# Eight of the 32 stencil groups summed by TensorE in a PSUM bank, the other 24 by VectorE

## What is computed

```
x = x + deformable_conv(group_norm(x))     # 8 groups of 16 channels, 9 sampling points per group
t = t + attention(layer_norm(t))           # 4 sequences of 1024 tokens
t = t + mixture_of_experts(layer_norm(t))  # top 2 of 8 experts, gelu
```

```
samples = _bilinear_sample(img, sg)        # at 9 offset points
out = (samples * m).sum(-1)                # m: softmax over the 9 points
return out @ out_w + out_b
```

## Time and profile before

| | |
|---|---|
| median of 3 runs | 685.37 us (684.22 to 685.88) |
| profiled execution, own time | 684.17 us |
| its span (first to last instruction) | 682.3 us |
| mean granted TensorE clock | 0.937 |
| busy: TensorE / VectorE / ScalarE / GpSimd | 86% / 83% / 34% / 50% |

### The profile page before, as it was taken

How to read it: one execution, slowest core, us unless ns; L and a number is a source line. 1 busy time by engine, 2 the same in 40 slices (tenths; PEclk the granted TensorE clock), 3 DMA queues, 4 the chain that set the end, 5 groups by cost and what they waited for, 6 DMA issues and landing times.

```text
span 682.3 us, 11125 instructions
## 1 busy us (share of the span) xinstructions
PE 587.8 (86%) x3518; PEld 435.4 (64%) x3518; DVE 565.8 (83%) x1028; ACT 234.0 (34%) x343; POOL 338.8 (50%) x407
## 2 busy tenths in 40 slices
PE   5989969888879588689786779999999999989995
PEld 4567556565556465466564667767777778775774
DVE  4679999999999699789999999956777667654877
ACT  6064405307116107006207000144454444414431
POOL 7505794888578658748667960201222121114222
PEclk9889959999899789969979889999999999999998
DMA  7096403003003006000000000000000000004111
GB/s 190 34 344 216 130 0 108 4 3 110 0 2 111 0 1 251 22 1 3 0 1 4 1 1 1 0 1 1 1 1 1 1 0 1 1 1 125 40 39 47
DMA packets 26238, 30.71 MB, mean 45 GB/s; under 512 B 5572, under 2 KB 18324, under 8 KB 26196
## 3 DMA queue, kind: packets, MB, share of 16 engines
q1 hardware_dynamic: 24094, 29.77, 13.3%
q0 software_dynamic: 1408, 0.36, 0.6%
q10 hardware_dynamic: 694, 0.01, 0.1%
HBM read 25.07 MB, written 5.05 MB: 44 GB/s over the span
## 4 chain that ended last, share of the span: by engine, by line
PE 38%; POOL 15%; DVE 15%; DMA 14%; issue 12%; POOLq 3%; ACT 1%; DVEq 1%; SPq 0%; ACTq 0%
DMA got<-padded,cell_now 11%; PE banks L1013 9%; PE pair L993 8%; DVE prod L1605 7%; POOL got L1258 6%; PE pair L1081 4%; PE banks L1003 4%; PE banks L1119 4%; PE banks L894 4%; DVE stencil L1546 2%; POOL cell_now L1254 2%; PE pair L838 2%; DMA padded<-stage 1%; POOL place L1337 1%; POOLq L1314 1%
## 5 line engine op out<-in xcount | busy, mean ns | idle before, releaser
L894 PE MATMUL banks<-ident,prod 128*128 128x128 f32 x1440 | 219.7, 295 | 63.5 <-DVE prod L1605 61.8
L894 PEld LDWEIGHTS banks<-ident,prod 128*128 128x128 f32 x1440 | 174.1, 150 | 125.3 <-DVE prod L1605 101.1
L1605 DVE TENSOR_TENSOR prod<-shifted,stencil 128x1024 f32 (+3 forms) x208 | 216.0, 1079 | 0.1
L1363 POOL TENSOR_TENSOR rstd_now<-mv_now,neg_half 128x2 f32<-128x2 f32 x32 | 23.0, 718 | 119.0 <-DVE mv_now L1656 119.0
L838 PE MATMUL pair<-xg,dw_diag 128*128 128x512 f32 x144 | 73.9, 614 | 1.4 <-DVE xg L1417 1.4
L1258 POOL DMA_INDIRECT got<-padded,cell_now x44 | 63.6, 1446 | 19.0 <-issue 10.1
L1013 PEld LDWEIGHTS banks<-shifted 128*128 128x128 f32 x512 | 60.2, 192 | 8.1 <-issue 6.1
L1013 PE MATMUL banks<-shifted 128*128 128x128 f32 x512 | 63.3, 277 | 2.3 <-ACT shifted L714 1.4
L993 PE MATMUL pair<-shifted 128*128 128x512 f32 x128 | 60.6, 596 | 0.1
L1671 DVE TENSOR_REDUCE neg_max<-pair 128x1 f32<-128x1024 f32 x32 | 39.2, 1224 | 23.1 <-PE pair L993 22.0
L1538 DVE TENSOR_TENSOR outer<-hats 128x800 f32<-128x800 f32 x56 | 56.1, 1001 | 1.2
(11 more groups left out here) (250 smaller groups left out, 920.7 us busy)
## 6 DMA issues: line engine op xcount, KB each, us to landing
shifted<-padded SPq DMA_DIRECT2D x42, 256.0 KB, 4.0
shifted<-padded SPq DMA_DIRECT2D x14, 640.0 KB, 8.5
res<-in_x_dram SPq DMA_DIRECT2D x4, 512.0 KB, 6.2
padded<-stage SPq DMA_DIRECT2D x4, 512.0 KB, 11.2
stage<-in_L_ffn_W_dram SPq DMA_DIRECT2D x16, 128.0 KB, 2.2
out_dram<-res SPq DMA_DIRECT2D x16, 128.0 KB, 1.8
got<-padded,cell_now POOLq DMA_INDIRECT x44, 3.0
padded<-stencil SPq DMA_DIRECT2D x2, 228.0 KB, 2.6
```

Source lines behind the costliest of these rows:

```text
L894: mm = pe.matmul(acc_of(c, r), prod[:, slot, r * G:(r + 1) * G, :].rearrange("p g c -> p (g c)"), ident[:, :], is_transpose=True, start=(t ...
L1605: ins = ve.tensor_tensor(prod[:, dx:dx + n, :, :], shifted[:, dx:dx + n, bass.ds(((c % HALF) * ROWS + dy) * G, ROWS * G), :], stencil_of[: ...
```

## The change

The groups 24 to 31 of a chunk (`SUMMED` = 8) are no longer added by VectorE. VectorE still computes all outer products, for all 32 groups. After each it waits for the product and raises `outer_done`; TensorE then adds the product of the eight groups into PSUM bank 2 with an fp32 matmul against the identity, at the window of the point (`sum_point`). In front of point 0 a matmul with a zero vector opens the bank. Each sum raises `outer_read`, which VectorE waits for before it writes `outer` again. When nine are done, ScalarE copies the bank into the stencil (`copy_sums`) and raises `stencil_summed`, and VectorE waits for that before the first product of the chunk. VectorE's adds cover 24 groups (`DIRECT`). The units that stood between product and add now stand behind the add. ScalarE clears 24 groups only.

```diff
 
 
 POINT_FILL = (1, 2, 2, 2, 2, 2, 2, 2, 2)
-STENCIL_FILL = (0, 0, 0, 0, 0, 0, 0, 0, 2)
+FIRST_POINT = BEGIN + 5
+POINT_UNIT = [FIRST_POINT + sum(POINT_FILL[:q]) for q in range(PTS)]
+SUMMED = 8
 
 EXP_AT = 4
 
...
         y_new = over_prod[:, 2:4, :].rearrange("p s (t c) -> p s t c", c=C)
         b2_rows = over_prod[:, 0, :].rearrange("p (n c) -> p n c", n=B)
         dense_t = over_prod[0:E, 1, :].rearrange("e (n t) -> e n t", n=B)
+
+        DIRECT = ROWS * G - SUMMED
+        size = ROWS * G * TAPS * TAPS
+        spare = prod[:, :, :, :].rearrange("p s g c -> p (s g c)")
+        first_outer = [outer[:, :, :, :]] + [spare[:, i * size:(i + 1) * size].rearrange("p (g a b) -> p g a b", a=TAPS, b=TAPS)
+                                             for i in range(3)]
+        summed = bank[2][:, 0:SUMMED * STENCIL]
 
         def key_bank(j):
 
...
 
             silu(0)
 
-            def prepare(k, exp_at=EXP_AT):
+            def copy_sums(k):
+                sc.wait_ge(outer_read, (k + 1) * PTS)
+                sc.sem_inc(act_waited, 1)
+                sc.activation(stencil[:, bass.ds(k % 2, 1), DIRECT * STENCIL:].rearrange("p s g -> p (s g)"),
+                              summed, ACT.Copy).then_inc(stencil_summed, 1)
+
+            def prepare(k, exp_at=EXP_AT, sums_at=TAPS):
 
                 sc.wait_ge(off_mm, k + 2)
                 if not isinstance(k, int) or k > 0:
...
                 sc.wait_ge(off_done, k + 1)
                 sc.sem_inc(act_waited, 1)
                 for t in range(TAPS):
+                    if t == sums_at:
+                        copy_sums(k - 1)
                     if t == exp_at:
                         sc.wait_ge(logits_done, k + 1)
                         sc.sem_inc(act_waited, 1)
...
 
                 sc.wait_ge(prod_done, (k + 1) * NEAR)
                 sc.sem_inc(act_waited, 1)
-                sc.activation(stencil[:, bass.ds(k % 2, 1), :].rearrange("p s g -> p (s g)"),
-                              zero_col[:, 0:1].to_broadcast([P, ROWS * G * STENCIL]), ACT.Copy
+                sc.activation(stencil[:, bass.ds(k % 2, 1), 0:DIRECT * STENCIL].rearrange("p s g -> p (s g)"),
+                              zero_col[:, 0:1].to_broadcast([P, DIRECT * STENCIL]), ACT.Copy
                               ).then_inc(stencil_clear, 1)
 
             def count_out(k):
...
             signs_of(0)
             silu(1)
             count_out(0)
+            copy_sums(0)
             prepare(1)
             signs_of(1)
             silu(2)
             count_out(1)
 
             def turn(j, conv_ahead):
-                prepare(j + 2)
+                prepare(j + 2, sums_at=3)
                 clear_stencil(j)
                 signs_of(j + 2)
                 if conv_ahead:
...
                               bank[at][:, n0 * P:n1 * P].rearrange("p (n c) -> p n c", c=C), ACT.Copy
                               ).then_inc(res1_first if n0 == 0 else res1_done, 1)
 
+            copy_sums(CHUNKS - 1)
             copy_out(CHUNKS - 2)
             copy_out(CHUNKS - 1)
             for i, k in enumerate((CHUNKS - 2, CHUNKS - 1)):
...
                                    start=False, stop=(i == 3))
                 mm.then_inc(far_mm, 1)
 
+            def sum_point(k, q):
+
+                kx, ky = q // 3, q % 3
+                if q == 0 and k > 0:
+                    pe.wait_ge(stencil_summed, k)
+                pe.wait_ge(outer_done, PTS * k + q + 1)
+                if q == 0:
+                    pe.matmul(summed, ones16[0:1, :], zero16[0:1, 0:1].to_broadcast([1, SUMMED * STENCIL]),
+                              start=True, stop=False)
+                    src = stencil_of[:, k % 2, DIRECT:, 0:TAPS, 0:TAPS]
+                else:
+                    src = (first_outer[q % 4] if k == 0 else outer)[:, DIRECT:, :, :]
+                pe.matmul(summed.rearrange("p (g a b) -> p g a b", a=WIN, b=WIN)[:, :, ky:ky + TAPS, kx:kx + TAPS],
+                          ident[:, :], src, start=False, stop=(q == PTS - 1)).then_inc(outer_read, 1)
+
             def acc_of(c, r):
                 return bank[1 + 2 * (c % 2)][:, r * P:(r + 1) * P]
 
...
             for t in range(9):
                 convolve(1, t)
             count_far(0)
-            keep_clock(20, bank[2])
+            for q in range(6):
+                sum_point(0, q)
+                keep_clock(4, bank[3])
             offsets(1, 0, ROWS)
-            keep_clock(14, bank[2])
+            for q in range(6, PTS):
+                sum_point(0, q)
+                keep_clock(3, bank[3])
             add_up(0, 0, first_of(BEGIN))
+
+            point_taps = [first_of(u) for u in POINT_UNIT]
 
             def turn(k, first, conv_ahead):
                 for i in range(first_of(BEGIN), NEAR):
...
                     r, between = divmod(i - AT_OFFSETS, 2)
                     if 0 <= r < ROWS and between == 0 and conv_ahead:
                         offsets(k + 2, r, r + 1)
+                    if i in point_taps:
+                        sum_point(k + 1, point_taps.index(i))
                     add_up(k, i, i + 1)
                 add_up(k, NEAR, NEAR + first_of(BEGIN))
 
...
                         list_far(k)
                     if q == AT_SILU and silu_next:
                         finish_silu(k + 1)
+                    if q > 0:
+                        ve.wait_ge(outer_read, PTS * k + (q if q > 1 else 0))
                     own(ve.tensor_tensor(to if q == 0 else outer[:, :, :, :],
                                          hy[:, :, q, :].unsqueeze(3).to_broadcast(full),
                                          hx[:, :, q, :].unsqueeze(2).to_broadcast(full), ALU.mult))
+                    own.wait()
+                    ve.sem_inc(outer_done, 1)
+                    if q == PTS - 1:
+                        ve.sem_inc(hats_used, 1)
+                    if q > 0:
+                        to = to[:, 0:DIRECT, :, :]
+                        own(ve.tensor_tensor(to, to, outer[:, 0:DIRECT, :, :], ALU.add))
                     fill(POINT_FILL[q])
-                    if q > 0:
-                        own.wait()
-                        if q == PTS - 1:
-                            ve.sem_inc(hats_used, 1)
-                        own(ve.tensor_tensor(to, to, outer[:, :, :, :], ALU.add))
-                        fill(STENCIL_FILL[q])
                 own.wait()
 
             def first_stencils():
...
                 point_product(1)
                 for q in range(1, PTS):
                     if q + 1 < PTS:
+                        if q >= 4:
+                            ve.wait_ge(outer_read, q - 2)
                         point_product(q + 1)
                         ve.wait_ge(dve, own.base + own.n - 1)
                     else:
                         own.wait()
                         ve.sem_inc(hats_used, 1)
+                    ve.sem_inc(outer_done, 2 if q == 1 else 1)
                     if q == AT_LIST:
                         list_far(0)
                     if q == AT_SILU:
                         finish_silu(1)
-                    own(ve.tensor_tensor(place_of_point(q), place_of_point(q), held[q % 4], ALU.add))
+                    to = place_of_point(q)[:, 0:DIRECT, :, :]
+                    own(ve.tensor_tensor(to, to, first_outer[q % 4][:, 0:DIRECT, :, :], ALU.add))
                 own.wait()
 
             def list_far(k):
...
                     full = [P, n, ROWS * G, CG]
                     if u == 0:
                         ve.wait_ge(rows_ready, c + 1)
+                        ve.wait_ge(stencil_summed, c + 1)
                     ve.wait_ge(prod_free, c * NEAR + max(freed_by(t), freed_by(t + n - 1)) + PROD)
                     ins = ve.tensor_tensor(
                         prod[:, dx:dx + n, :, :],
```

11 lines of the change are left out of this document (6 added, 5 removed).

## The result

| | before | after |
|---|---|---|
| median of 4 runs each | 684.92 us (684.22 to 685.88) | 694.06 us (692.58 to 695.48) |
| ratio, 95% interval | | 1.014, 1.0121 to 1.0159 |
| span of the profiled execution | 682.3 us | 690.7 us |
| VectorE's MAX8 for chunks 0 / 5 / 7 starts at | 54.61 / 292.11 / 387.81 | 52.84 / 295.98 / 396.39 |
| GpSimd takes the list of chunk 4 | 290.31 | 276.17 |

The forecast was 685.0 us (681.0 to 690.5). The change is slower, and by more than the range allowed.

What follows compares the result with a forecast made beforehand. GpSimd was taken to bound the stage before 292 us, VectorE alone from there to 435. VectorE's +1.4 us and GpSimd's -1.8 gave -0.4 us: from the median 685.4 to 685.0 us, range 681 to 690.5.

Steps and rivals of the forecast that it cites:

- What bounds before: Deformable convolution: GpSimd's far points are the clock before 292 us, VectorE alone from there to 435 us.
- The adds: VectorE's adds over 24 groups: 0.21 us less each, eight adds in each of eight chunks.
- The new order: VectorE, add directly behind its product: exposed gap 0.13 us instead of 0.03, so a point saves 0.11 us net.
- the row with one additional wait: Profile row of VectorE's gap before the gate, 0.13 us, taken as the gap between product and add.
- The wait at the chunk's end: VectorE's first product of a chunk waits for ScalarE's copy: about 1.8 us in turns 0 to 5, ends 1.0 and 3.
- waits for TensorE in the loop: VectorE waiting for TensorE before outer products in the loop: named as making the forecast wrong, given no size.
- The sum of a turn: A full VectorE turn: 0.9 us shorter from adds and order, 1.8 us longer from the wait for the copy.
- The start: Chunk 0: sums replace filler matmuls, VectorE's first product starts 4 us later, weighing of the hats +5.4 us.
- Where VectorE meets the lists: VectorE 1.9 us late at the first far-point list, 3.2 us of waiting left at the second; sum +1.4 us.
- GpSimd's own path: GpSimd's steps beside VectorE's new gaps and idle time: -1.8 us, at least 3 us uncertain either side.
- The rivals: Alternatives to the forecast of no change: slower, 688 to 691 us, chance 0.31; faster, 680 to 683 us, chance 0.29.
- The slower one: TensorE's sums become the bound, chunk-end wait 3 us instead of 1.8: 688 to 691 us, chance 0.31.

Runs made afterwards that it cites:

- tenth experiment: The kernel before with only VectorE's adds cut to 24 groups, old order, the other eight groups' sums left out: 679.0 us, ratio 0.9918.
- first experiment: The changed kernel, but ScalarE copies the summed groups before its copy of the offsets: 679.5 us, ratio 0.9927 to the kernel before.

## Why the prediction was wrong, step by step

**What bounds before: right.** The tenth experiment turned the saving on the adds into list waits as the prediction read them.

**The adds: right.** 0.80 us against 0.99; 0.78 was forecast. VectorE's groups by form, 90 to 396 us of after (busy, mean ns | idle in front):

```profile
L1596 DVE TENSOR_TENSOR stencil<-stencil,outer 128x600 f32 x40 | 31.9, 799 | 10.4 <-DVE outer L1587 10.4
```

**The new order: the step that failed first.** The prediction took the gap from "the row with one additional wait", 0.13 us. The edit puts a wait and an increment there, and both are exposed: 0.25 us. The two are now apart by runs in all four combinations: a wait alone is 0.04 us in written-out turns and 0.15 in the loop (where a register instruction stands in it too), with the increment 0.15 and 0.25. The prediction's row, 0.13, was the wait alone in the loop. The difference, 0.12 us, is 1.0 us a loop turn; at point 0 the gap is 0.46 instead of 0.2. The Trainium skill (VectorE: DVE Perf Modes, The DRAIN you can't avoid) reports a chain of copies that took the same time with a semaphore after each instruction as with one at the end. The exposed sequence here is not free: the fourth kernel, in which the order is the only edit, is slower than before by 0.12 to 0.35%.

**The wait at the chunk's end: right in mechanism, a little small.** 12.0 us in six turns, 2.0 each, against 1.8 and a range of 1.0 to 3. The chain is the one forecast: offset matmuls, offsets copy, three absolute values, copy. Taking it away (first experiment) gave 13.2 us by the profiled spans, a little more than these 12.0.

**Not counted: waits for TensorE in the loop.** VectorE waited 2.1 us in front of outer products (`outer_read`) and 1.0 us for freed product slots (the 1.5 us of the view hold one 0.45 us gap behind point 0, which has that length in every loop turn), some 0.5 us a turn together. The prediction named the first as something that would make it wrong, and priced it at nothing.

**The sum of a turn: +0.9 us forecast, +3.2 measured.** Between the second and the last MAX8 after needs 306.3 us and before 287.1 without its list waits: 19.3 us in six turns. The copy waits are 2.0 us of the 3.2, against 1.8 forecast. The waits for TensorE are 0.5, against nothing. The new order with the shorter adds costs some 0.7, where a saving of 0.9 was forecast: of these 1.6 us the gaps behind the products are 0.9 and the one behind point 0 is 0.2; the rest has no single place. So the exchange of one exposed dependence for another, priced at 0.10 us a point, is the term that was mis-sized, and it turned the adds' saving into a loss.

**The start: too large.** Forecast +5.4 us to the weighing of the hats. It came at 73.61 against 72.33; counted from the first MAX8, which was 1.8 us earlier in this execution, +3.0 us. TensorE's sums with fillers, from its timeline:

```profile
49.78 0.33 PE L914 MATMUL banks<-zero,ones 1*128 1x392 bf16 x1
50.05 0.61 PE L919 MATMUL banks<-stencil,ident 128*128 128x200 f32 x2
50.50 1.05 PE L829 MATMUL banks<-ident 128*128 128x128 f32 x8
51.39 0.50 PE L919 MATMUL banks<-prod,ident 128*128 128x200 f32 x2
...
57.55 0.53 PE L853 MATMUL pair<-offmask_w,gate 128*128 128x216 f32 x2
```

A sum with its fillers takes 1.23 us (1.39 forecast), and the six began at 49.8, not at 52.5: the offset matmuls start at their old time, 57.5.

**Where VectorE meets the lists: the step on which the sign hung.** With +0.9 us a turn the prediction brought VectorE 1.9 us late to the first list and left 3.2 us of waiting at the second. With the measured 3.2 us a turn it is at its fifth MAX8 at 245.7, where 240.4 was forecast, and at its sixth at 295.98, behind the old 292.11, which the prediction said it would keep. From there no microsecond of the new cost is hidden.

**GpSimd's own path: wrong in size, without effect.** Forecast -1.8 us with at least 3 either way; it was -14.1. The direction of the mechanism can be seen at point 0, whose gap now is 0.46 us. VectorE, then GpSimd, in after:

```profile
230.68 1.00 DVE L1587 TENSOR_TENSOR stencil<-hats 128x800 f32 x1
232.15 1.22 DVE L1655 TENSOR_TENSOR prod<-shifted,stencil 128x1024 f32 x1 [0.46 <-DVE stencil L1587]
```

```profile
230.86 0.88 POOL L1291 TENSOR_TENSOR pos<-got_off,got_here 128x8 f32<-128x8 f32 x1 [0.56 <-POOL got_here L1284]
231.71 0.21 POOL L1292 TENSOR_TENSOR cell_f<-corner,got_here 128x16 f32<-128x16 f32 x1
232.00 0.19 POOL L1294 TENSOR_SCALAR pos<-pos 128x8 f32<-128x8 f32 x1
232.28 1.21 POOL L1295 TENSOR_SCALAR low<-pos 128x8 f32<-128x8 f32 x1
```

The first and the last of these steps end just behind a VectorE instruction; the two that fall into its gap take 0.2 us. The prediction held a gap of 0.13 us too short for that; how much of the 14 us such places gave is not shown. As VectorE had become the clock, nothing of the 14 us reached the time.

**The rivals.** The slower one had the right side, 688 to 691 us, and a wrong cause: the wait for the copy was 2.0 us and not 3, and TensorE's granted clock was 0.96 in the stretch where it had been 0.83. That the list waits would go came true. Its 688 to 691 is 3.8 to 7 us on top of the profiled 684.2; from the median 685.4, from which the forecast starts, it would be 689.2 to 692.4. Either way it stops short of 694, because it kept the turn at the prediction's gap.
